# A transformer block on one core: the probability tails of two heads stacked by DMA, and loads in pieces behind the moves

## The reference

```python
h = layernorm(x)                                  # x (2, 1024, 256), ctx (2, 154, 256)
q, k, v = h @ Wq + bq, ctx @ Wk + bk, ctx @ Wv + bv   # 16 heads of 64
p = softmax(where(mask, -1e30, q @ k.T / 8))      # (2, 16, 1024, 154)
x = x + (p @ v) @ Wo + bo
y = layernorm(x) * g + b                          # second half: 16 experts of 64 slots
se = (layernorm(slot_embeds) * slot_g + slot_b) * scale
logits = einsum("bnd,esd->bnes", y, se)
slots = einsum("bnd,bnes->besd", y, softmax(logits, over n))
eout = (gelu(slots @ Wg + bg) * (slots @ Wu + bu)) @ Wd + bd
x = x + softmax(logits, over e, s) @ eout
```

## Time and profile before

| | us |
|---|---|
| runs | 544.94, 543.82, 544.62 |
| median | 544.62 |
| profiled execution | 544.24 |
| its span | 542.5 |
| PE busy | 530.0 (98%) |
| DVE busy | 434.1 (80%) |
| ACT busy | 402.2 (74%) |
| POOL busy | 303.3 (56%) |
| attention, one stretch of four steps | 31.7 |

### The profile page before, as it was taken

How to read it: one execution, slowest core, us unless ns; L and a number is a source line. 1 busy time by engine, 2 the same in 40 slices (tenths; PEclk the granted TensorE clock), 3 DMA queues, 4 the chain that set the end, 5 groups by cost and what they waited for, 6 DMA issues and landing times.

```text
span 542.5 us, 11967 instructions
## 1 busy us (share of the span) xinstructions
PE 530.0 (98%) x3896; PEld 499.8 (92%) x3896; DVE 434.1 (80%) x1305; ACT 402.2 (74%) x1098; POOL 303.3 (56%) x327
## 2 busy tenths in 40 slices
PE   6999999999999999999998999999999999999997
PEld 4889999999999999999997888999978888899997
DVE  6777878787897979899677998798699888865453
ACT  5879969596896959779564555788979889766562
POOL 6674654544545455454365768787467999910000
DMA  8635000000030000000001333150288888525551
GB/s 257 181 86 179 3 1 2 2 2 1 3 98 2 2 2 1 2 0 4 0 1 80 155 156 156 78 201 1 79 264 283 270 306 288 182 79 170 181 167 67
DMA packets 34901, 54.11 MB, mean 100 GB/s; under 512 B 3997, under 2 KB 21497, under 8 KB 34713
## 3 DMA queue, kind: packets, MB, share of 16 engines
q1 hardware_dynamic: 34841, 53.36, 29.7%
HBM read 40.54 MB, written 10.49 MB: 94 GB/s over the span
## 4 chain that ended last, share of the span: by engine, by line
PE 90%; ACT 4%; DMA 2%; POOL 1%; DVE 1%; issue 1%; SPq 0%; ACTq 0%; DVEq 0%
PE ps L1461 9%; PE ps L1585 9%; PE ps L1357 9%; PE ps L1369 8%; PE ps L1610 8%; PE ps L1499 8%; PE ps L1439 7%; PE ps L1552 7%; PE ps L1476 5%; PE ps L1632 4%; PE ps L1501 4%; PE ps L1644 3%; DMA wvo_raw<-in_L_xattn_Wo_dram 2%; ACT expo L885 1%; PE ps L1615 1%; PE ps L1622 1%
## 5 line engine op out<-in xcount | busy, mean ns | idle before, releaser
L885 ACT ACTIVATE expo<-expo,nmin 128x154 f32<-128x154 f32 x256 | 106.2, 423 | 5.3 <-DVE nmin L1135 4.8
L1135 DVE CUSTOM_DVE_ANT_0 expo<-ps,maskb 128x154 f32<-128x154 f32 x256 | 69.1, 312 | 11.9 <-PE ps L1461 11.9
L723 POOL TENSOR_TENSOR prob_t<-expo,prec 128x104 f32<-128x104 f32 x64 | 23.1, 360 | 89.3 <-DVE prec L1146 89.1
L726 POOL TENSOR_TENSOR prob<-expo,prec 128x512 f32<-128x512 f32 x64 | 66.8, 1043 | 0.0
L1461 PE MATMUL ps<-kbd,qT_high 128*128 128x308 f32 x256 | 61.1, 323 | 0.0
L1155 DVE TENSOR_TENSOR pT_low<-ps,pT_high 128x512 fp32r<-128x512 f32 (+1 forms) x96 | 57.2, 596 | 4.1 <-ACT pT_high L899 3.9
L788 POOL TENSOR_TENSOR w_gu_low<-w_raw,w_gu_high 128x1024 fp32r<-128x1024 f32 x17 | 50.3, 2966 | 16.2 <-ACT w_gu_high L835 16.1
L899 ACT CAST pT_high<-ps 128x512 fp32r<-128x512 f32 (+1 forms) x96 | 49.1, 513 | 10.8 <-PE ps L1476 8.1
L803 ACT ACTIVATE oT_high<-ps,bqv_c 128x256 fp32r<-128x256 f32 x64 | 29.8, 466 | 34.8 <-PE ps L1501 34.7
L885 ACT ACTIVATION_READ_ACCUMULATOR expo<-expo,nmin 128x1 f32 x256 | 50.3, 196 | 0.0
L1461 PEld LDWEIGHTS ps<-kbd,qT_high 128*128 128x128 f32 x256 | 39.8, 190 | 0.2
(11 more groups left out here) (241 smaller groups left out, 1762.7 us busy)
## 6 DMA issues: line engine op xcount, KB each, us to landing
logits_dram<-lsb SPq DMA_DIRECT2D x16, 512.0 KB, 2.6
w_raw<-in_L_ffn_Wg_dram SPq DMA_DIRECT2D x16, 512.0 KB, 4.0
w_raw<-in_L_ffn_Wu_dram SPq DMA_DIRECT2D x16, 512.0 KB, 4.5
w_raw<-in_L_ffn_Wd_dram SPq DMA_DIRECT2D x16, 512.0 KB, 4.5
lraw<-logits_dram SPq DMA_DIRECT2D x13, 512.0 KB, 3.8
out_dram<-gate SPq DMA_DIRECT2D x16, 128.0 KB, 2.2
kbd<-keys SPq DMA_DIRECT2D x12, 154.0 KB, 2.8
wvo_raw<-in_L_xattn_Wv_dram SPq DMA_DIRECT2D x2, 512.0 KB, 7.0
```

What stands on the lines that cost most here:

```text
L726: pool.tensor_tensor(prob[:, n % 2, :, heads, :], expo[:, n % 2, pp, :, :, 0:P], prec[:, n % 2, pp].unsqueeze(3).to_broadcast([P, 2, 2, P] ...
L885: ins = act.activation(row, row, ACT.Exp, scale=-1.0, bias=nmin[:, n % 2, pp, j, h:h + 1], accum_out=psums[:, n % 2, pp, j, h:h + 1])
L1135: ins = dve.tensor_tensor_reduce(out=expo[:, n % 2, pp, j, h, :], in0=ps[:, s % NS, h * SK:(h + 1) * SK], in1=maskb[:, (2 * (n // QUADS) + ...
```

## The change

1. **Stacked tails.** `prob_t` has 64 columns for a head pair: 52 probabilities and 12 zeros (a memset by DVE once). T (n, 2) is then two transposes of 128 × 128, and its halves are `tT_high` and `tT_low`, 128 rows by 256 (64 rows a pair, one buffer). SP moves them with four DMAs of 64 KB a step (`place_tails`): the high halves after ACT, the low ones after DVE, so that `tS[:, n % 2, pp]` has the high half of pair pp on 64 partitions and its low half on the other 64. `vt` holds the values of a pair twice, once for either. One matmul of 128 rows then does high and low of the probabilities at once: v_high and v_low against the stack are two matmuls, and low × low is computed too. PV has six matmuls of mains, then waits for the DMAs of T (n, 2) (`d_tt`, 64 a step), then the two of the tails: eight in all. ACT waits for the DMAs of the step before it writes `tT_high` anew.
2. **Loads in pieces.** `vt` takes four DMAs for batch 0 and, later, four for batch 1. Wo comes in four pieces of 256 KB, x's second half in four of 256 KB, the slot embeddings in eight of 128 KB. Three such pieces go out behind the move of each T2 (`PIECES_A_MOVE`). The buffer `tails` lies in x's second half, so the loads there wait for the moves out of it.
3. **Order.** `STEP` is new, and so are `PROLOGUE`, `LOADS`, `EARLY` and the tables of shifts; `WK` 1 is loaded last, and the two splits of Wo come at T (3, 2). Two small tasks of the logits stage (`SA`, `SB`) are put in ahead of the Q events one step later.

On PE, in the steady attention, this is one PV before. The names are the operands: `pT` the probabilities' mains, `vm` the values' mains, `vt` the tail values.

The diff, cut to its core:

```diff
-    ("x",), ("split", WK, 0), ("split", WQ, 0), ("bias",), ("split", WK, 1), ("split", WV, 1),
-    ("split", WK, 2), ("split", WV, 0), ("mask",), ("split", WQ, 1), ("split", WQ, 2),
+    ("split", WK, 0), ("x",), ("split", WQ, 0), ("bias",), ("split", WQ, 1), ("split", WV, 1), ("mask",),
+    ("split", WK, 2), ("split", WQ, 2), ("split", WV, 0), ("split", WK, 1),
...
-STEP = "R1 S00 S01 PV0 T0 LN R0 PV1 Q0 XN S10 Q1 T2 S11 T1 xT0 Y0 xT1 Y1"
...
+STEP = "R1 S00 S01 Q0 PV0 T2 S10 R0 LN Q1 S11 T0 XN xT0 xT1 PV1 T1 Y0 Y1"
...
+    "SA": 3.5, ("split", WK, 2): -6.5, "S00": -2.5, "T2": -1.5, "S10": -3.0, "Y1": 2.0, "R0": -2.5, "T1": 0.5,
...
-N2_AT = 19
-YA_AT = {(0, 0): 26, (1, 0): 26, (0, 1): 28, (1, 1): 29}
+LATER_POOL = {'Y1': 2.5, ("split", WQ, 1): -4}
+N2_AT = 8
+YA_AT = {(0, 0): 25, (1, 0): 30, (0, 1): 33, (1, 1): 30}
 A_LATE = 3
+PIECES_A_MOVE = {"K": 0, "VT": 0, "Q": 0, "T": 3}
...
-        head.insert(head.index(("S", GROUPS // B * QUADS + 1 + k + (k >= ST // 2), 0, 0)), ev)
+        head.insert(head.index(("Q", GROUPS // B * QUADS + 2 + k + (k >= ST // 2), 1)), ev)
...
+    second_at = -(-nc.sbuf_base // 32) * 32 + 4 * TB * D
     x1 = sb(top, "x1", [P, TILES, D])
+    tails = nc.alloc_sbuf_tensor_at("tails", [B * TAIL, 2, DM], F32R, offset=second_at)
...
-    vt = sb(att, "vt", [T4, B, 2, QUADS, 4 * DH], F32R)
+    vt = sb(att, "vt", [P, B, 2, PAIRS, P], F32R)
...
-    prob_t = sb(att, "prob_t", [P, 2, 2, 4, TAIL])
+    prob_t = sb(att, "prob_t", [P, 2, 2, 2, DH])
...
-    tails = sb(pro, "tails", [B * TAIL, 2, DM], F32R)
     pro.close()
     loop = ExitStack()
-    pT = halves(loop, "pT", [P, 2, 5, 2 * P])
+    pT = halves(loop, "pT", [P, 2, 4, 2 * P])
+    tT = halves(loop, "tT", [P, 2 * P])
+    tS = sb(loop, "tS", [P, 2, 2, 2 * P], F32R)
...
-        elif n == 2:
-            for b in range(B):
-                eng.wait_ge(d_tails[b], 16 * 4)
...
-        for ev in [ev for ev in first if ev in placed_no or ev == LAST_VT]:
+        def place_values(b, a):
+            for twice in range(2):
+                at = twice * DH + a * TAIL
+                sp.dma_start(vt[at:at + TAIL, b, :, :, a * DH:(a + 1) * DH]
+                             .rearrange("p s q d -> p (s q) d").bitcast(F32),
+                             tails[b * TAIL:(b + 1) * TAIL].rearrange("p s (q a d) -> p (s q) a d", a=2, d=DH)
+                             [:, :, a, :].bitcast(F32)).then_inc(d_tails[b], 16)
+        def place_keys(ev):
             wait_used(sp, ev)
+            for h in range(2):
+                at = slice(h * DH, (h + 1) * DH)
+                sp.dma_start(kbd[at, :, :, ev[1], h * SK:(h + 1) * SK].rearrange("p b s k -> p (b s) k").bitcast(F32),
+                             keys[at, placed_no[ev] % NK].rearrange("p b s k -> p (b s) k").bitcast(F32)).then_inc(d_keys[ev], 16)
+        def place_tails(ev):
+            for half, done in ((0, t_high), (1, t_free)):
+                sp.wait_ge(done, t_no[ev] + 1)
+                for pp in range(2):
+                    to = pp ^ half
+                    sp.dma_start(tS[to * DH:(to + 1) * DH, ev[1] % 2, pp].bitcast(F32), tT[half][pp * DH:(pp + 1) * DH].bitcast(F32))\
+                        .then_inc(d_tt, 16)
+        moves = [ev for ev in before_ffn if ev in placed_no or ev == LAST_VT or ev[0] == "T" and ev[2] == 2]
+        se_at = moves.index(("T", GROUPS // B * QUADS - 2, 2))
+        def load_part(kind, k):
+            if kind == "vt":
+                place_values(1, k)
+            elif kind == "x":
+                if k == 0:
+                    for b in range(B):
+                        sp.wait_ge(d_tails[b], 16 * 4)
+                sp.dma_start(x1[:, TB + 2 * k:TB + 2 * k + 2], x_t[:, 1, 2 * k:2 * k + 2]).then_inc(d_x_second, 16)
+            elif kind == "gain":
+                sp.dma_start(gain[:], norm_g.unsqueeze(0).to_broadcast([P, D])).then_inc(d_gain, 16)
+                sp.dma_start(shift[:], norm_b.unsqueeze(0).to_broadcast([P, D])).then_inc(d_gain, 16)
+            elif kind == "wo":
+                at = slice(2 * k, 2 * k + 2)
+                sp.dma_start(wo[2][:, at], Wo.rearrange("(k p) n -> p k n", p=P)[:, at]).then_inc(d_w[WO][0], 16)
+            elif k is None:
+                sp.dma_start(sg_b[:], slot_g.unsqueeze(0).to_broadcast([P, D])).then_inc(d_se, 16)
+                sp.dma_start(sb_b[:], slot_b.unsqueeze(0).to_broadcast([P, D])).then_inc(d_se, 16)
+                sp.dma_start(sc_b[:], scale.unsqueeze(0).to_broadcast([P, 1])).then_inc(d_se, 16)
+            else:
+                sp.dma_start(se[:, k], slot_embeds.rearrange("(t e) s d -> (e s) t d", e=P // SLOTS)[:, k]).then_inc(d_se, 16)
+        rest, wo_asked = [], False
+        for at, ev in enumerate(moves):
             if ev == LAST_VT:
-                sp.wait_ge(vt_zeros, 2)
-                for b in range(B):
-                    for a in range(4):
-                        sp.dma_start(vt[a * TAIL:(a + 1) * TAIL, b, :, :, a * DH:(a + 1) * DH]
-                                     .rearrange("p s q d -> p (s q) d").bitcast(F32),
-                                     tails[b * TAIL:(b + 1) * TAIL].rearrange("p s (q a d) -> p (s q) a d", a=4, d=DH)
-                                     [:, :, a, :].bitcast(F32)).then_inc(d_tails[b], 16)
+                wait_used(sp, LAST_VT)
+                sp.wait_ge(vt_zeros, 3)
+                for a in range(2):
+                    place_values(0, a)
+            elif ev[0] == "K":
+                place_keys(ev)
             else:
-                for h in range(2):
-                    at = slice(h * DH, (h + 1) * DH)
-                    sp.dma_start(kbd[at, :, :, ev[1], h * SK:(h + 1) * SK].rearrange("p b s k -> p (b s) k").bitcast(F32),
-                                 keys[at, placed_no[ev] % NK].rearrange("p b s k -> p (b s) k").bitcast(F32)).then_inc(d_keys[ev], 16)
-        sp.dma_start(x1[:, TB:TILES], x_t[:, 1]).then_inc(d_x_second, 16)
-        sp.dma_start(gain[:], norm_g.unsqueeze(0).to_broadcast([P, D])).then_inc(d_gain, 16)
-        sp.dma_start(shift[:], norm_b.unsqueeze(0).to_broadcast([P, D])).then_inc(d_gain, 16)
-        wait_done(sp, LAST_V)
-        sp.dma_start(wo[2], Wo.rearrange("(k p) n -> p k n", p=P)).then_inc(d_w[WO][0], 16)
-        sp.wait_ge(s_full, s_no[("S", GROUPS // B * QUADS - 1, 1, 1)] + 1)
-        sp.dma_start(se[:], slot_embeds.rearrange("(t e) s d -> (e s) t d", e=P // SLOTS)).then_inc(d_se, 16)
-        sp.dma_start(sg_b[:], slot_g.unsqueeze(0).to_broadcast([P, D])).then_inc(d_se, 16)
-        sp.dma_start(sb_b[:], slot_b.unsqueeze(0).to_broadcast([P, D])).then_inc(d_se, 16)
-        sp.dma_start(sc_b[:], scale.unsqueeze(0).to_broadcast([P, 1])).then_inc(d_se, 16)
+                place_tails(ev)
+            if before_ffn.index(ev) > before_ffn.index(LAST_V) and not wo_asked:
+                wait_done(sp, LAST_V)
+                wo_asked = True
+                rest = [("wo", k) for k in range(PAIRS // 2)] + [("vt", a) for a in range(2)] + \
+                    [("x", k) for k in range(TB // 2)] + [("gain", 0)]
+            if at == se_at:
+                sp.wait_ge(s_full, s_no[("S", GROUPS // B * QUADS - 1, 1, 1)] + 1)
+                rest = [("se", None)] + [("se", t) for t in range(ST)] + rest
+            for piece in rest[:PIECES_A_MOVE[ev[0]]]:
+                load_part(*piece)
+            rest = rest[PIECES_A_MOVE[ev[0]]:]
+        assert not rest
...
-                pool.tensor_tensor(prob_t[:, n % 2, :, heads, :], expo[:, n % 2, pp, :, :, P:SK],
+                pool.tensor_tensor(prob_t[:, n % 2, :, pp, 0:T2].rearrange("p j (h k) -> p j h k", h=2), expo[:, n % 2, pp, :, :, P:SK],
...
-            if i != WO or c == 0:
-                act.wait_ge(d_w[i][c], 16)
+            act.wait_ge(*((d_w[i][0], 8 * PAIRS) if i == WO else (d_w[i][c], 16)))
...
-                rows, tiles = (P, 2) if t < 2 else (T4, 1)
-                act.copy(pT[0][0:rows, n % 2, 2 * t:2 * t + tiles],
-                         ps[0:rows, NS + k % NT, 0:tiles * 2 * P].rearrange("p (t n) -> p t n", t=tiles))\
+                if t == 2 and n:
+
+                    act.wait_ge(d_tt, 64 * n)
+                dst, tiles = (pT[0][:, n % 2, 2 * t:2 * t + 2], 2) if t < 2 else (tT[0][:].unsqueeze(1), 1)
+                act.copy(dst, ps[:, NS + k % NT, 0:tiles * 2 * P].rearrange("p (t n) -> p t n", t=tiles))\
...
+        dve.memset(prob_t[:, :, :, :, T2:DH].rearrange("p n j q k -> p (n j q) k"), 0.0).then_inc(vt_zeros, 1)
...
+                dst, high, tiles = [half[:, n % 2, 2 * t:2 * t + 2] for half in (pT[1], pT[0])] + [2] if t < 2 else \
+                    [tT[1][:].unsqueeze(1), tT[0][:].unsqueeze(1), 1]
+                dve.tensor_tensor(dst, ps[:, NS + k % NT, 0:tiles * 2 * P].rearrange("p (t n) -> p t n", t=tiles),
+                                  high, ALU.subtract).then_inc(t_free, 1)
...
-                        ins = pe.transpose(ps[0:T4, NS + k % NT, j * P:(j + 1) * P],
```

(14 more changed lines are left out.)

95 lines of the change are left out of this document (47 added, 48 removed).

## The result

The changed kernel takes 547.24 us (median of 18 runs, 545.39 to 551.51) beside 544.54 us for the kernel before (18 runs, 543.65 to 545.23): ratio 1.006, interval 1.0045 to 1.0076. It is slower, where I had forecast 539.6 and given slower 0.07.

The account below looks back on a forecast made before the run. PE was taken as the bound, busy 530.0 of 542.5 us. The terms summed to −5.0, from 544.24 to 539.2 us for the profiled execution, 539.6 for the median; range 536.8 to 543.5.

Parts of the forecast that it names:

- A: Attention's PVs: eight matmuls instead of nine, 64 PVs at 0.12 us each, −7.7 us.
- B: Tail transposes in the attention: 128 rows wide instead of 104, 32 × 0.05, +1.6 us.
- D: Prologue: WK 1 loaded last makes the third K start later, +1.3 us, bounds 0 and +1.8.
- F: End of the attention: PE's wait for x2f with the second norm earlier, 0 us, bounds −0.6 and +0.8.
- G: Steps without Y: ACT, nearly as long as PE, delays them a little, +0.7 us, bounds 0 and +4.6.
- its rival: First rival: ACT becomes the bound in the 24 steps without Y, total only −1.1, 543.5 us; chance 0.12.
- C: Attention's first steps: Wo in pieces lands sooner, removing PE's waits, −1.1 us, bounds 0 and −1.1.
- E: First PV: fewer, larger DMAs of the tails' values, then tail moves, tight timing, +0.2 us, bounds 0 and +1.
- My own sign of being wrong: Attention's first steps: a start more than 2 us later would show the prediction wrong.
- H: Tail moves in each step: in place 4.9 us after T2's start, wanted after 5.95, margin 1.1 us, cost 0.
- the third rival: Tail moves land late, at 4.3 us, so PE waits in PV0 of each step: 549.2 us; chance 0.08.

Follow-up runs that it names:

- the 64 matmuls: Changed kernel with 64 one-column matmuls added in the gap at PE's start: 545.00 us, range 544.22 to 548.51.
- the last two kernels: Changed kernel with 64 one-column start matmuls, one piece a move, later mask: 546.45 us; the same with WK 1's load at its old place: 545.13 us.
- a whole packet more: Kernel before with 132 one-column matmuls replacing the four warming ones at PE's start, 256 PE instructions more: 545.71 us, range 545.20 to 546.25.
- the three edits at once: Changed kernel with one piece of x behind a move, the mask's conversion later and N2_AT 19 again: 554.09 us (1.0152 to 1.0215).

## Why the prediction was wrong

**A** had the right price: 0.12 us a matmul, seen wherever PE waits for nothing (−2.23 in steps 8 to 16). That it would reach the end in all 32 steps is what failed, below. **B** is nothing: from the tail transposes to the next instruction it is 0.14 us (115.24 to 115.38) where it was 0.13, not 0.18. And the new order gives 0.04 a step that I had not counted (31.58 against 31.72 for four steps with nine matmuls). Together −0.28 a step instead of −0.19.

**D** had the right size, +1.42 for +1.3, by luck. WK 1 landed at 15.41, 0.6 earlier than forecast, and the K started at 18.00, 0.5 later. In between stood DVE: it copied the mask (1.73 us where it took 0.79 before), finished the second key block and made the low half of WK 1 only at 17.17, without a pause ahead of it. With the mask later the low half came at 16.19, the K at 17.03, and step 2 at +1.04. With the load at its old place besides, and the 64 matmuls, step 2 was at +0.96. So the load's place was worth 0.1 by these two; it was worth 2.1 between the last two kernels, where WK 1 landed at 16.46 and 1.0 us of DVE's time passed in waiting for it. About 1.0 of the 1.42 goes with the new order of the prologue, which no run took apart.

**F** was not 0. From step 31 to x2f lie the PVs of three steps, worth −0.8, and −0.10 was measured: +0.7, inside the bound of +0.8. The wait is the one of 1.22 on oT_low at 275.88; PE's idle time in the stretch ahead of x2f rose from 0.92 to 1.62 us.

**G** failed, and its rival with it. ACT was busy for 6.04 of 6.38 us and is now for all of 6.08, and PE waits for it nowhere. A busy share near 1 of an engine that runs ahead is not a bound; I had taken it for one.

**C and E** failed in the same way: both treated a wait as an amount to take off. The wait for Wo went, and others came behind it. ACT now casts Wo ahead of the tail's copy, so DVE's half of the tail is late (1.12 at 61.28; 0.17 with the cast behind it), and so is the move (1.69 at 65.88, of which 1.1 are a packet of instructions). With the 1.06 at 43.59 that is 3.9 us of waits, for 1.06 before. My own sign of being wrong, first steps more than 2 us late, came true (+3.07 at the first S, +2.92 at step 3).

**H** held in the steady state, and by two errors that cancel. From T2's start to the last landing it was 4.8 us where I had 4.9. But the landing was 1.9/2.0/3.5 us for the 2.8 I took, and the four DMAs took some 0.6 us each to issue, one behind the other, for my 0.33 in all behind DVE's half. PE waited for no move between 66 and 285 us, so the third rival did not come. H failed for steps 0 and 3, where the first move left late: 5.5 us after T2's start in step 0, since SP was issuing into vt until 39.57, and 4.0 in step 3, for 0.96 in a steady step. My margin of 1.1 us was that of a steady step.

**The largest step is one that the prediction did not have**: in the second half the gain of A has DVE's norms in its way. The row stood in the earlier trace rows: DVE 28.77 of 31.71 us, more than ACT's 25.20. I had asked which engine is second in a step of the first half only. With 1.1 us taken out of four steps DVE has under 2 us left there, and in the new order SA and SB fall beside POOL's product and get longer. At −0.28 a step steps 16 to 31 should have gained 4.2 us and lost 0.35: 4.5 us. SB is 2.5 of it by the run on 8 columns. Another 0.9 falls in steps 16 to 20 and comes from the loads in pieces: the last piece of the slot embeddings lands at 165.6, where the whole stood ready at 153.3 before, so DVE waits 1.84 us for se and PE then 0.43 at 170.36. The kernel without moves gains 1.10 in these four steps and the one with the 64 matmuls 0.94, for 0.23 in the changed one. Another 0.9 falls in steps 20 to 24, which gain 0.24 instead of 1.1 even with the small SB; PE waits 0.6 us on xT_low there from 207.15 on. Here the Trainium skill had a rule that speaks against the change, and I had not weighed it: "SBUF — State Buffer", section "Who interferes with whom", says that a DVE instruction with two SBUF inputs contends with a GpSimd instruction that reads SBUF. The trace agrees: 0.48 alone, 1.15 beside POOL. SB has two such inputs (se and sb_b), and where it lands relative to POOL's product changed with the order and the tables of shifts.

**The last part lies outside all that was changed**: 1.4 us of the median in the expert stage (2.7 less the 1.3 at x2f). With the instructions put back 0.2 of it is left (0.4 less 0.2 at x2f), so it goes with the shifted stream of 16 KB packets. Nothing that I had read of the kernel before said that this stage is unstable: its load of Wu at 434 lands 0.1 us before it is used.

Added up against the forecast, at x2f: the steps −3.6 (32 steps at −0.28, −9.0, where A, B and G gave −5.4), C and E +4.5 (from step 2 to step 8 +1.90 where −0.28 a step gives −1.7, so +3.6, where I had −0.9), D +0.1, the second half +4.5, F +0.7: +6.2, which is from −5.0 to +1.3 but for rounding. The part behind the attention makes +2.7 of it.

## What to carry to other kernels

Look for the second engine in every kind of stretch, the last one too, and not in the one from which the prices come; an engine at 91% there is the next bound once PE gets 4% faster. A wait that is removed at the head of a pipeline only moves on until something in the chain behind it has slack, so follow it for two more steps. When a term comes out at the right size, look at its rows before calling it right: D and H were sums of parts that were each wrong. When a kernel's runs scatter more than before, compare a short and a long run where the code is unchanged, and shift it by some tens of small instructions before any stage is blamed.

## What the runs showed of the hardware

- **Instruction fetch reaches the data loads.** A 16 KB packet on q8 beside the issue of a 512 KB load went with an issue of 0.6 to 1.4 us instead of 0.42 and a landing of 5.5 us instead of 4.5 (medians; 7.1 at most), in 21 loads of the 20 traces. It does not do so always: the profiled run of the changed kernel has a packet 0.95 us ahead of the load, and 0.52 us, and many loads with a packet beside them took 0.37. Nor does it always cost time: the kernel before with a whole packet more has an issue of 1.23 us at 445.57, and no run above 546.25. The 64 KB moves are hit too: all seven of the changed kernel that landed after more than 2.7 us have a packet beside them. By what mechanism a packet of that size delays a DMA stays open. That the packets are PE's was worked out from their distance and borne out by the shift, not shown by a label.
- **DVE and POOL on SBUF.** Of two operations with two SBUF inputs that overlap, one waits for the other: 0.48 becomes 1.15 on DVE beside 1.04 that becomes 1.32 on POOL. Of the 128x1024 halves, in two pairs, the one that starts first keeps its pace. In the kernel before DVE is first by 0.11 us, and takes 1.24, its shortest there, to POOL's 3.40:

```profile
440.00 1.24 DVE L1043 TENSOR_TENSOR w_gu_low<-w_raw,w_gu_high 128x1024 fp32r<-128x1024 f32 x1
```
```profile
440.11 3.40 POOL L788 TENSOR_TENSOR w_gu_low<-w_raw,w_gu_high 128x1024 fp32r<-128x1024 f32 x1
```

  In the rows from 450.21 above POOL is first by 0.12 us, and takes 2.40, its shortest, to DVE's 3.36. Columns matter little then: SB on 8 columns still took up to 0.93 us, for 0.23 without POOL beside it.
- **An idle of 3 us costs more than 3 us.** After the wait of 2.97 us the granted clock was 0.87 and 0.79 in the stretches from 440 and 450, that is partly the lower of its two levels (1.2 and 2.4 GHz), and PE ran 50 matmuls in 10 us instead of 60. After the waits of 1.12 and 1.69 us in the changed kernel it stayed at 1.00, and so it did after the single wait of 2.46 in the kernel before with moves:

```profile
61.00:66.00 5.00, 3.04 (x23) 2.83 (x24) 4.22 (x19) 4.25 (x17) 4.64 (x5) 1.00 0.44 117
66.00:70.00 4.00, 4.00 (x34) 4.00 (x35) 2.10 (x11) 3.58 (x13) 0.98 (x2) 1.00 0.61 173
```

  Shorter waits close together were followed by the lower clock in some runs and not in others. With Wo's cast later, behind 1.72 and 1.54 us, the same stretch had 0.57 and 14 matmuls instead of 34, with 1.0 us of it idle. With the norms under Y the clock fell at 67.3 us behind 1.11 and 1.97; with the three edits at once it did not fall behind 1.11 and 2.14:

```profile
66.00:70.00 4.00, 2.97 (x14) 3.00 (x15) 1.56 (x10) 1.42 (x7) 1.88 (x3) 0.57 0.25 78
```

- **Small moves inside SBUF are quick, and still not free.** 128 DMAs of 64 KB landed in 1.9/2.0/3.5 us, and in the old order, where no engine but SP waits for them, the steps are 31.7 us with and without. In the new order the kernel that issues them without PE's wait is 3.2 us behind the one without them at x2f.
